# A selective scan whose start state is folded into the first column of its input

## What is computed

```python
dt  = softplus(einsum(dt_low, dt_w) + dt_b)
dA  = exp(dt[..., None] * A)                     # decay, one per channel and state
dBx = (dt * xi)[..., None] * B[:, :, None, :]    # share, u = dt * xi
def step(h, inp):
    a, bx, c = inp
    h = a * h + bx
    return h, einsum('bds,bs->bd', h, c)         # y sums h*C over the states
_, ys = scan(step, zeros, (dA, dBx, C))
```

## Time and profile before

| what | value |
|---|---|
| time, median of 3 runs | 4762.65 us (4761.55 to 4768.12) |
| profiled execution, its span | 4760.7 us; the profile gives no other time of that execution |
| PE busy | 4479.5 us (94%) |
| VectorE busy | 3894.2 us (82%) |
| ScalarE busy | 3109.7 us (65%) |
| GpSimd busy | 3320.9 us (70%) |
| scan stage | first scan 81.5 us, last scan begins 3424.7 us |

### The profile page before, as it was taken

How to read it: one execution, slowest core, us unless ns; L and a number is a source line. 1 busy time by engine, 2 the same in 40 slices (tenths; PEclk the granted TensorE clock), 3 DMA queues, 4 the chain that set the end, 5 groups by cost and what they waited for, 6 DMA issues and landing times. The chain is left out here.

```text
span 4760.7 us, 67108 instructions
## 1 busy us (share of the span) xinstructions
PE 4479.5 (94%) x24932; PEld 3395.1 (71%) x24932; DVE 3894.2 (82%) x4126; ACT 3109.7 (65%) x5158; POOL 3320.9 (70%) x1559
## 2 busy tenths in 40 slices
PE   7999999999999989999999999998799999999999
PEld 3666666666666666667666667666688888888888
DVE  5999999999999999999999999999854444444452
ACT  6777777777777777777777777777444444444443
POOL 4999999999999999999999999999820000000000
PEclk9999999999999999999999999999999999999999
DMA  7544444444444444444444444444231111010100
GB/s 271 178 142 141 134 151 132 136 134 134 143 139 134 155 132 138 129 139 139 131 147 140 129 130 136 143 142 156 103 123 32 36 32 36 32 36 32 36 23 10
DMA packets 297736, 545.76 MB, mean 115 GB/s; under 512 B 101888, under 2 KB 186624, under 8 KB 262784
## 3 DMA queue, kind: packets, MB, share of 16 engines
q1 hardware_dynamic: 296512, 529.91, 35.6%
q10 hardware_dynamic: 896, 11.54, 0.7%
HBM read 502.77 MB, written 50.14 MB: 116 GB/s over the span
## 5 line engine op out<-in xcount | busy, mean ns | idle before, releaser
L1400 DVE TENSOR_TENSOR_SCAN m_h<-bank,m_state,m_dBx 128x512 f32<-128x512 f32 x1512 | 1841.2, 1265 | 35.0 <-ACT bank L1145 27.2
L868 PEld LDWEIGHTS bank<-ident,m_h 128*128 128x128 f32 x8192 | 980.9, 143 | 417.2 <-issue 345.8
L868 PE MATMUL bank<-ident,m_h 128*128 128x128 f32 x8192 | 1197.6, 276 | 12.9 <-DVE m_h L1408 12.8
L1283 POOL TENSOR_TENSOR m_dBx<-u,m_Bs 128x1024 f32<-128x1024 f32 x432 | 1016.4, 2377 | 0.4 <-DMA m_Bs<-b_dram 0.2
L1283 POOL TENSOR_TENSOR m_dBx<-m_u,m_Bs 128x1024 f32<-128x1024 f32 x432 | 1015.5, 2371 | 1.2 <-DMA m_Bs<-b_dram 1.0
L1294 POOL TENSOR_TENSOR m_h<-m_h,m_Cs 128x1024 f32<-128x1024 f32 x384 | 909.4, 2368 | 105.8 <-ACT m_state L1077 105.1
L1408 DVE TENSOR_TENSOR m_h<-m_h,bank 128x1024 f32<-128x1024 f32 x640 | 767.0, 1198 | 51.7 <-PE bank L850 51.4
L1145 ACT ACTIVATE bank<-m_dt,cols 128x512 f32<-128x512 f32 x864 | 584.8, 688 | 225.2 <-DVE m_h L1400 223.7
L1145 ACT ACTIVATE bank<-dt,cols 128x512 f32<-128x512 f32 x864 | 584.1, 688 | 193.6 <-DVE m_h L1400 191.6
L302 POOL TENSOR_TENSOR mvj<-mvj,norm_c 128x4 f32<-128x4 f32 x16 | 16.5, 1032 | 969.0 <-DVE mvj L263 969.0
L731 PE MATMUL bank<-hT,w_in 128*128 128x512 f32 x1024 | 547.4, 630 | 113.1 <-ACT hT L998 105.8
(11 more groups left out here) (177 smaller groups left out, 5847.1 us busy)
## 6 DMA issues: line engine op xcount, KB each, us to landing
m_Bs<-b_dram SPq DMA_DIRECT2D x256, 1024.0 KB, 6.3
m_Cs<-c_dram SPq DMA_DIRECT2D x384, 256.0 KB, 3.7
m_dg<-d_dram SPq DMA_DIRECT2D x160, 256.0 KB, 3.9
xx<-in_x SPq DMA_DIRECT2D x16, 512.0 KB, 4.9
xn_dram<-xx SPq DMA_DIRECT2D x16, 512.0 KB, 4.5
yb_dram<-m_ysb SPq DMA_DIRECT2D x16, 512.0 KB, 5.0
xx<-xn_dram SPq DMA_DIRECT2D x16, 512.0 KB, 3.8
x_dram<-m_ysb SPq DMA_DIRECT2D x16, 512.0 KB, 5.0
```

What stands on the lines that cost most here:

```text
L868: mm = pe.matmul(YB[b][:, o:o + P], h[:, k % NH, m, tok:tok + P], ident[:, :], start=(s == 0 and o == 0), stop=False, is_transpose=True, s ...
L1283: pool.tensor_tensor(dBx[:, dbx_ring(ch, k) % NDBX, :, :], u[ch.batch][:, m, :], Bs[:, k // BP % 2, k % BP, :].unsqueeze(1).broadcast_to(( ...
L1400: dve.tensor_tensor_scan(o, decays, share, initial, ALU.mult, ALU.add).then_inc(S["scan"], 1)
```

## The change

It replaces the scans' start value for the 27 units of B_UNITS in carried chunks. A scan that begins from h0 has a first value a0 * h0 + u0 * B0. That sum is now put into the first column of the share tile (column 0, in pass 0 the last, `edge_col`), and the scan begins from 0.0: a0 times 0 plus that column. The five A_UNITS keep the state.

- GpSimd (`weigh_b`): the product leaves out that column: 2 x 511 columns in place of 2 x 512.
- TensorE (`front` at AT_C): one more small transposing matmul broadcasts B's column of 16 states to 128 partitions.
- ScalarE: a copy of it to `B_edge`; `edge_decay`, four Exp of 128x16 a chunk, two at step 26 (second half of this chunk) and two at step 61 (first half of the next), for a0; `put_edge`, 14 copies a chunk of the edge values of two units (the last of one) into `dBx`, 128x4 each, ahead of the decay of the first unit of the pair.
- VectorE (`carry`): behind scan 26 (second half) and behind scan 60 (first half of the next chunk): edge = a0 * state, 128x32, a wait for that on its own semaphore, then twice edge = B_edge * u0 + edge, 128x16 each.

```diff
+PAIRS = tuple(B_UNITS[i:i + 2] for i in range(0, NBU, 2))
+NPAIR = len(PAIRS)
+AT_A0 = (61, 26)
+AT_EDGE = (60, 26)
...
+        B_edge = sb("B_edge", [P, DS])
+        edge = sb("edge", [P, NU, 2])
...
+                    if not ch.opens():                                   # TensorE, front
+                        t = edge_col(ch)
+                        mm = pe.matmul(FB[BANK[J_C]][:, TS * rows:TS * rows + DS],
+                                       dbB[B0:B0 + DS, t:t + 1].broadcast_to((DS, P)), ident[B0:B0 + DS, B0:B0 + DS],
+                                       start=True, stop=True, is_transpose=True)
...
+            def edge_decay(ch, half):                                    # ScalarE
+                q, t = ch.batch, edge_col(ch)
+                act.wait_ge(S["dt_done"], ch.at(2, half + 1))
+                wait(act, S["edge_put"], NPAIR * ch.carried())
+                for m in (2 * half, 2 * half + 1):
+                    col = COL_A + m * DS
+                    ins = act.activation(edge[:, half * DS:(half + 1) * DS, m - 2 * half], cols[:, ch.ps, col:col + DS],
+                                         ACT.Exp, scale=dt[q][:, m, t:t + 1])
+                ins.then_inc(S["a0"], 1)
...
+            def put_edge(ch, k):                                         # ScalarE, ahead of decay(ch, 2 * k)
+                for pair in PAIRS:
+                    if pair[0] != k:
+                        continue
+                    t = edge_col(ch)
+                    held = unit(ch, B_UNITS[made(pair[-1]) - NDBX] - (NU if made(pair[-1]) < NDBX else 0))
+                    act.wait_ge(S["scan"], held[0].at(STEPS, 2 * held[1] + 2))
+                    act.wait_ge(S["edge"], 2 * ch.carried() + pair[-1] // DS + 1)
...
+                    act.copy(dst, src).then_inc(S["edge_put"], 1)
...
-                pool.tensor_tensor(dBx[:, dbx_ring(ch, k) % NDBX, :, :], u[ch.batch][:, m, :],
-                                   Bs[:, k // BP % 2, k % BP, :].unsqueeze(1).broadcast_to((P, 2, T)),
+                t = slice(0, T) if ch.opens() else slice(0, T - 1) if rev(ch) else slice(1, T)
+                n = t.stop - t.start
+                pool.tensor_tensor(dBx[:, dbx_ring(ch, k) % NDBX, :, t], u[ch.batch][:, m, t],
+                                   Bs[:, k // BP % 2, k % BP, t].unsqueeze(1).broadcast_to((P, 2, n)),
                                    ALU.mult).then_inc(S["dbx"], 1)
...
-                initial = 0.0 if ch.opens() else state[:, q, k, m:m + 1]
+                initial = 0.0 if ch.opens() or k in B_UNITS else state[:, q, k, m:m + 1]
...
+            def carry(ch, half):                                         # VectorE
+                q, t, n = ch.batch, edge_col(ch), 2 * ch.carried() + half + 1
+                units = slice(half * DS, (half + 1) * DS)
+                dve.wait_ge(S["a0"], n)
+                dve.tensor_tensor(edge[:, units, :], edge[:, units, :], state[:, q, units, :], ALU.mult
+                                  ).then_inc(S["edge_mul"], 1)
+                wait_drained(dve, ch, J_C)
+                dve.sem_inc(S["go"], 1)
+                dve.wait_ge(S["u_ready"], ch.at(2, half + 1))
+                dve.sem_inc(S["go"], 1)
+                dve.wait_ge(S["edge_mul"], n)
+                for m in range(2):
+                    ins = dve.scalar_tensor_tensor(out=edge[:, units, m], in0=B_edge[:, :],
+                                                   scalar=u[q][:, 2 * half + m, t:t + 1], in1=edge[:, units, m],
+                                                   op0=ALU.mult, op1=ALU.add)
+                ins.then_inc(S["edge"], 1)
...
                         scan(ch, k, m)
+                        if g == AT_EDGE[1] and carries(ch, 0):
+                            carry(ch, 1)
+                        if g == AT_EDGE[0] and carries(ch, 1):
+                            carry(ch.go(1), 0)
```

More of the change, by code:

```diff
@@ L119, in opens, with carried @@
         return isinstance(self.c, int) and self.c == 0
+    def carried(self):
+        n = self.number()
+        return n - min(n, BATCH) - min(max(n - NCH, 0), BATCH)
     def at(self, per_chunk, off):
@@ L199 @@
     "sp_exp", "sp_ln", "dt_done", "u_ready", "b_st", "b_in0", "b_in1", "c_in0", "c_in1", "da", "dbx", "scan", "save",
-    "c_fill", "d_zero", "d_init", "d_st", "d_in0", "d_in1", "a_fill", "weigh_d", "weigh_p", "turned", "skip", "y_turned", "y_evac",
+    "c_fill", "a0", "edge_mul", "edge", "edge_put", "d_zero", "d_init", "d_st", "d_in0", "d_in1", "a_fill", "weigh_d", "weigh_p", "turned", "skip", "y_turned", "y_evac",
     "y_out", "xn_in", "xn_out",
@@ L409, in flip, with edge_col, carries @@
             return slice(None, None, -1) if rev(ch) else slice(None)
+        def edge_col(ch):
+            return T - 1 if rev(ch) else 0
+        def carries(ch, k):
+            return has(ch, k) and not ch.go(k).opens()
         def has(ch, k):
@@ L1039, in front @@
                     wait_filled(act, ch, J_C)
+                    if not ch.opens():
+                        wait(act, S["edge"], 2 * ch.carried())
+                        act.copy(B_edge[:, :], FB[BANK[J_C]][:, TS * rows:TS * rows + DS])
                     turned = FB[BANK[J_C]][:, 0:TS * rows].rearrange("p (t s) -> p t s", s=rows)
@@ L1071, in scale_skip @@
                                        ).then_inc(S["skip"], 1)
+            def edge_decay(ch, half):
[15 more added lines that the diff above has]
+                    act.wait_ge(S["edge"], 2 * ch.carried() + pair[-1] // DS + 1)
+                    a = dbx_ring(ch, pair[0]) % NDBX
+                    if len(pair) == 1:
+                        dst, src = dBx[:, a, :, t], edge[:, k, :]
+                    else:
+                        b = dbx_ring(ch, pair[1]) % NDBX
+                        dst = dBx[:, a:b + 1, :, t] if b > a else dBx[:, a::b - a, :, t]
+                        src = edge[:, k:pair[1] + 1:pair[1] - k, :]
+                    act.copy(dst, src).then_inc(S["edge_put"], 1)
             def keep_state(ch, p):
@@ L1180, in body @@
                 for k in range(STEPS):
+                    if k % 2 == 0 and carries(ch, 0):
+                        put_edge(ch, k // 2)
                     decay(ch, k)
+                    if k == AT_A0[1] and carries(ch, 0):
+                        edge_decay(ch, 1)
+                    if k == AT_A0[0] and carries(ch, 1):
+                        edge_decay(ch.go(1), 0)
                     if ch.first() and k % 2 == 0 and k // 2 < len(copies):
```

## The result

The changed kernel takes 5011.35 us (4998.91 to 5028.5, four runs), the kernel before 4762.98 (4761.55 to 4768.12) beside it: 1.0521 times as long, 95% interval 1.0493 to 1.0549. Forecast: 5025, range 4870 to 5115. The profiled execution has a span of 5026.6 us, 265.9 over the one before.

The account below looks back on a forecast made before the run. VectorE was taken to set the pace in the scan stage, GpSimd close behind. 4760.7 - 89 (saving) + 365 (stall) + 11 (puts) - 25 (waits for C) = 5022.7, the median 2 us over the span: predicted 5025 us, range 4870 to 5115.

Parts of the forecast that it names:

- The stop and its cause: Behind scans 26 and 60 of carried chunks, added VectorE instructions with two SBUF inputs wait for GpSimd; slower, chance 0.85.
- rival C: At the same two stops, the small instructions slip between GpSimd's reads, costing 31 us; kernel 4716 us, chance 0.13.
- The stall, 365 us: Behind scans 26 and 60, each added instruction waits for one GpSimd instruction: 12.6 to 13.5 us a chunk, 365 in all.
- the 1 to 3 us named beforehand: Under strict alternation, the added 128x32 product has a mean of 1 to 3 us, each 128x16 group over 2 us.
- D: Behind scan 60 mostly, GpSimd keeps the ports through a back-to-back run, giving way only when waiting: 5155 us, chance 0.06.
- A: The forecast itself: VectorE and GpSimd strictly alternate at both stops, each 4.7 to 7.6 us; 4940 to 5095, chance 0.62.
- The 0.13 us read at the feed-forward: Where the feed-forward begins, a held VectorE instruction's wait ends some 0.13 us before GpSimd's instruction does.
- The saving, 89 us: The 1512 GpSimd-fed scans in carried chunks begin from 0, each 58.9 ns shorter: 89 us less.
- GpSimd's floor: Opening chunks of pass 1, 100.95 us each with GpSimd busy, limit any gain to about 2.5 us a chunk.
- Idle time, +11 - 25: ScalarE's puts ahead of decays add 11 us; half of VectorE's 51.4 us wait for C goes, 25 us back.
- GpSimd's products stay where they were: GpSimd's products, losing one column in 512, keep their duration: taken as 0, bounds -4 to +7 us.
- the chunks of 112 to 113 us: In the changed profile, carried chunks would last 112 to 113 us.

Follow-up runs that it names:

- e1: Changed kernel with VectorE's three added instructions at each stop replaced by sum reductions with one SBUF input, all waits kept: 4750.88 us.
- e3: Kernel before plus only VectorE's three added instructions at the same two stops, on scratch tiles that nothing else reads: 5007.13 us.
- e2: Kernel before with the scans of the 27 units begun from 0.0 in all chunks, their state not carried, nothing else changed: 4724.74 us.
- e6: Changed kernel with TensorE's transposes of C for units 10 and 26 done seven times, so it has work while VectorE is held: 5010.56 us.
- e7: Changed kernel without VectorE's added instructions; its waits, ScalarE's Exps, copies and puts and GpSimd's 511 columns stay: 4739.4 us.
- e5: Changed kernel in which GpSimd waits for its own last instruction at a few steps around scans 26 and 60: 4888.64 us.
- e4: Changed kernel, complete, with the edge sum moved from VectorE to GpSimd's own queue as three operations of 128x32 at each stop: 4747.44 us.

## Why the prediction was right, and where not

**The stop and its cause: right.** The time went into three small VectorE instructions, because both tensor inputs are in SBUF (e1: without the second input, 4751; e3: they alone, 5007). Sign and place were as forecast, and rival C is out: the 168 take 1.5 us each on average, where C needed waits under 0.28.

**The stall, 365 us: mis-sized; it is 252.5.** The step that failed is "the product of 128x32 waits for the one in flight, the first scalar-tensor-tensor for the next, the second for the last". In 26 of the 28 stops behind scan 26, and in 4 behind scan 60, the product waits for GpSimd's whole run and the pair then passes in 0.5 us. Its group has a mean of 3392 ns, over the 1 to 3 us named beforehand, and the pair's 783 and 418 ns where "over 2 us" was asked of each. That is D's mechanism, given 0.06. A's turns hold for the pair alone (13 of 16 ends), and it seldom has to wait. Behind scan 26 the price was 146 us against 200: the run ended about 5 us behind the scan and not 6.7 or 7.6, as the phase was reckoned. Behind scan 60 it was 109 against 165, since I took GpSimd's three instructions as one run, as they stood in the rows. In the changed kernel GpSimd paused behind the first in 21 of 28, waiting for B's DMA, in 15 of them long enough for all three. Of the 7 stops where it didn't pause, 5 took 10.3 to 10.6 us; D had that in every chunk for its 5155.

The Trainium skill, page "SBUF — State Buffer", sections "Who interferes with whom" and "Summary: rules for kernel authors", says that the engine that issues second is fully blocked until the first one's instruction is over. The trace agrees on the full block, whatever the size: 10.22 us for 32 values a partition. It differs on the end: at 61 of 78 ends of an instruction whose successor had begun, VectorE was not let in, and the measurement decides. The 0.13 us read at the feed-forward held: the shortest product takes 0.17 us, and one that waited ended 0.05 us behind GpSimd's instruction, so its wait ended some 0.12 us before it.

**The saving, 89 us: right in busy time, wrong in time.** I counted 58.9 ns x 1512 in full, since VectorE sets the pace. The scans' groups fell by 79 in the changed kernel and by 89 in e2, but e2 gained 38 us. My check was against GpSimd's floor alone (2.5 us a chunk). I did not look at the decays and TensorE's shares, for which VectorE then waited longer.

**Idle time, +11 - 25: wrong in sign.** VectorE's idle time rose by 92 us: 38 of it for decays (55.0 to 93.2), 20 for TensorE's shares and 19 for C (51.4 to 70.8, in place of the halving). Part of it belongs to the saving: the shortened scans alone add 45 us (e2), the stops alone 36 (e3). I let the stall give TensorE time; it also let TensorE run dry, and the clock fell (0.98 to 0.95), which I had priced at nothing. In e6, with the clock back, idle time over 26 chunks is 47 us less, and over the kernel it is 45 above the kernel before, as in e2. That points to the clock for the stops' part; it doesn't prove it, as said there. ScalarE's 15 us (e7 over e2) were near the 11.

**The sum**, 5022.7 for a profiled execution of 5026.6 (the median is 15 us below it), came out because the errors offset: 112 too much for the stall, against 106 too little for idle time and 10 for the saving in the changed kernel. That nearness is luck and confirms none of the terms. That GpSimd's products stay where they were was right: 2399 and 2362 ns, before 2377. GpSimd's idle time of over 10 us a chunk came as said; the chunks of 112 to 113 us came in pass 1 (112.7), not in pass 0 (115.7). Two slips in the working decided nothing: ScalarE's idle time is 25.8 us a chunk, not 24.5, and stalls of 4.7 to 7.6 us give A a range of 4923 to 5086, not 4940 to 5095.

**Left open:** why the product passes nearly every end of overlapping GpSimd instructions while the pair behind it gets in at most. No run separates the kind of instruction from its place behind a turn of VectorE's. In e3 and e6 it is the same: the product got in at 4 of 44 and 13 of 77, the pair at 11 of 14 and 20 of 23. Open too: why GpSimd has to wait for B's DMA behind scan 60 so much oftener than in the kernel before, and what the clock costs by itself.

## What to carry to other kernels

A VectorE instruction whose two tensor inputs are in SBUF can cost, beside a busy GpSimd, what is left of GpSimd's run and not its own size. Put such small work in GpSimd's own queue (252.5 us became 43 and the kernel faster), or keep one input out of SBUF. A reduction with one input wasn't held either (e1); not every one-input instruction is safe, though: the tensor-scalar of 128x4 took 0.50 us beside GpSimd. Letting GpSimd wait for itself just there took 122 us off, but that kernel is still 2.7% slower than the one before. And a shortened instruction is worth its busy time only up to the next wait: one run of the saving alone would have shown 38 us for 89.

## What was not expected of the hardware

- GpSimd's instructions overlap by 0.03 to 0.1 us when nothing is waited for. At such an end a waiting product was kept out in 58 of 62 cases, and a break of 0.18 us lets two small instructions in (e5). Nine waits more a chunk on GpSimd made the kernel 122 us faster.
- A scan with start 0.0 takes 1203 to 1207 ns, one with a value per partition 1265: about 60 ns for the operand.
- A held VectorE leaves TensorE without work and its clock low for the time after: 0.00 us of TensorE work and a clock of 0.56 in the 6 us around the end of the stop, then 0.59 with 4.80 us of work.
- GpSimd's product or sum of 128x32 takes 0.25 to 0.26 us (e4), so the three at a stop cost less than one wait for a GpSimd instruction of 2.4 us.
